# The order of TensorE's products and combines in layers 1 to 4 of a five-layer graph network on one core

## The reference, cut to what matters

```python
x = _layernorm(x + _L0_gnn_ref(x, adj, ...))            # layer 0: adj masked and weighted by rank
def _ggc(x, adj, W, wih, whh, bih, bhh):                # layers 1 and 2
    m = adj @ (x @ W)
    gi = m @ wih.T + bih
    gh = x @ whh.T + bhh
    ...
    r = jax.nn.sigmoid(i_r + h_r); z = jax.nn.sigmoid(i_z + h_z)
    n = jnp.tanh(i_n + r * h_n)
    return (1.0 - z) * n + z * x
x = _layernorm(x + relu(_ggc(relu(_ggc(x, ...)), ...)))
x = _layernorm(x + (dinv[:, None] * (adj + eye) * dinv[None, :]) @ x @ W)          # layer 3
x = _layernorm(x + concat([x, (adj @ x) / deg], -1) @ W.T)                          # layer 4
```

## Time and profile before

| | |
|---|---|
| median of 3 runs | 458.71 us (458.45 to 458.75) |
| time of the profiled execution | 457.77 us |
| its span, first to last instruction | 456.0 us |
| mean granted TensorE clock | 0.985 of full |
| PE busy | 428.1 us, 94% of the span |
| DVE, ACT, POOL busy | 283.2, 197.8, 114.9 us |

### The profile page before, as it was taken

How to read it: one execution, slowest core, us unless ns; L and a number is a source line. 1 busy time by engine, 2 the same in 40 slices (tenths; PEclk the granted TensorE clock), 3 DMA queues, 4 the chain that set the end, 5 groups by cost and what they waited for, 6 DMA issues and landing times.

```text
span 456.0 us, 6313 instructions
## 1 busy us (share of the span) xinstructions
PE 428.1 (94%) x2294; PEld 214.0 (47%) x2294; DVE 283.2 (62%) x777; ACT 197.8 (43%) x335; POOL 114.9 (25%) x155
## 2 busy tenths in 40 slices
PE   5399799999999999999999999999999999999992
PEld 1134244444344444455555545554545655465571
DVE  3575969666964896463667526868742566175453
ACT  2277567766876687506555414445111121100000
POOL 8111614210510020014122111343330444211011
PEclk9889999999999999999999999999999999999997
DMA  8999999999999991000011010000000111101000
GB/s 117 155 163 108 107 107 107 109 113 110 107 110 112 109 99 25 0 7 18 13 24 24 13 23 1 2 1 0 2 0 1 23 24 24 24 12 36 12 13 23
DMA packets 24895, 23.70 MB, mean 52 GB/s; under 512 B 14369, under 2 KB 16289, under 8 KB 24865
## 3 DMA queue, kind: packets, MB, share of 16 engines
q0 software_dynamic: 9360, 16.78, 36.7%
q1 hardware_dynamic: 15216, 6.33, 5.8%
q10 hardware_dynamic: 288, 0.20, 0.2%
HBM read 69.44 MB, written 1.05 MB: 155 GB/s over the span
## 4 chain that ended last, share of the span: by engine, by line
PE 85%; DVE 6%; DMA 3%; ACT 2%; issue 2%; POOL 1%; POOLq 0%; DVEq 0%; ACTq 0%
PE Y L887 46%; PE both L800 17%; PE Y L779 8%; PE Y L791 3%; PE both L760 2%; PE both L763 2%; DMA xrow<-in_xrow 2%; DVE work L550 2%; PE both L755 2%; PE both L766 1%; PE both L807 1%; PE both L768 1%; DMA adjT<-in_adjT 1%; ACT wgt L353 1%; DVE work L555 1%
## 5 line engine op out<-in xcount | busy, mean ns | idle before, releaser
L887 PE MATMUL Y<-adjT,S 128*128 128x512 fp8e4 (+1 forms) x1056 | 232.7, 373 | 1.0 <-POOL S L252 0.7
L887 PEld LDWEIGHTS Y<-adjT,S 128*128 128x128 f16 x1056 | 102.8, 99 | 110.2 <-POOL S L252 1.2
L353 ACT ACTIVATE wgt<-both 128x512 int16<-128x512 f32 x192 | 113.9, 597 | 44.3 <-PE both L800 36.8
L237 POOL TENSOR_TENSOR rstd<-stat,mhalf 128x4 f32<-128x4 f32 (+2 forms) x29 | 34.0, 1173 | 195.0 <-DVE stat L457 195.0
L800 PE MATMUL both<-adjT,fix 128*128 128x512 fp8e4 x192 | 73.8, 384 | 1.0 <-ACT wgt L353 0.5
L800 PE MATMUL both<-adjT,tri 128*128 128x512 fp8e4 x192 | 74.2, 387 | 0.0
L779 PE MATMUL Y<-wgt,S 128*128 128x512 bf16 x192 | 73.8, 384 | 0.0
L265 POOL DMA_DIRECT2D adjT<-in_adjT x63 | 33.7, 570 | 68.3 <-DMA adjT<-in_adjT 68.3
L550 DVE SCALAR_TENSOR_TENSOR work<-work,adjT 128x1024 int16<-128x1024 int16 x32 | 42.7, 1356 | 0.0
L555 DVE SCALAR_TENSOR_TENSOR work<-adjT,work 128x1024 int16<-128x1024 fp8e4 x24 | 29.4, 1225 | 16.7 <-ACT work L350 15.0
L800 PEld LDWEIGHTS both<-adjT,fix 128*128 128x128 bf16 x192 | 18.9, 98 | 38.8 <-ACT wgt L353 17.8
(11 more groups left out here) (112 smaller groups left out, 422.1 us busy)
## 6 DMA issues: line engine op xcount, KB each, us to landing
adjT<-in_adjT POOLq DMA_DIRECT2D x63, 256.0 KB, 39.0
out_rows<-xrow SPq DMA_DIRECT2D x7, 128.0 KB, 1.9
xrow<-in_xrow SPq DMA_DIRECT2D x1, 640.0 KB, 8.7
hrow<-in_w_gates SPq DMA_DIRECT2D x1, 512.0 KB, 13.5
biases<-in_biases SPq DMA_DIRECT2D x1, 416.0 KB, 7.7
x<-S SPq DMA_TRANSPOSE x24, 2.4
xrow<-in_xrow SPq DMA_DIRECT2D x1, 256.0 KB, 4.1
adjT<-in_adjT POOLq DMA_DIRECT2D x2, 128.0 KB, 6.3
```

The source lines that it names most:

```text
L237: nc.gpsimd.tensor_tensor(rstd[:, 0:blocks], stat[:, 2, 0:blocks], mhalf[:, 0:blocks], ALU.pow)\
L353: nc.scalar.activation(wgt[:, c, tiles % 2, :], V[c][:, :], ACT.Relu).then_inc(w_ready[c], 1)
L887: mm = nc.tensor.matmul(bank(layer, g)[:, 0:nb * P], S[layer % 2][:, jb, :], cols[:, jb, :], start=(jb == 0), stop=(jb == JB - 1), skip_gr ...
```

## The change

The four functions that write out PE's order are replaced. The products and combines in them are the same; their order differs.

- In layer 0's tail and the start of layer 1, `combine(0, 6)` comes first and `combine(0, 7)` one slot later, where both stood behind seven slots. `open_gates` comes after 30 more slots instead of 41.
- In layers 1 and 2 each combine of group g stands 13 to 15 slots behind the last slot of the same group's product (19 and 23 for groups 1 and 2 of layer 1); in the kernel before it stands 12 to 66 slots behind. In layer 3 it stands 4 slots behind, with two exceptions at the start, in layer 4 mostly 4 instead of 6.
- At the layer changes two groups (two banks) are open while the last rows of `S` are awaited, and a third is begun, where before three or four groups were open.
- At the end, `combine(4, 6)` and `combine(4, 7)` stand 8 and 6 half-width slots into the next group, where both stood 10.

```diff
             def layer1():
-                product(1, 2, 0, 7)
-                combine(0, G - 2)
-                combine(0, G - 1)
-                product(1, 2, 7, EARLY)
-                product(1, 3, 0, EARLY)
+                combine(0, 6)
+                product(1, 2, 0, 1)
+                combine(0, 7)
+                product(1, 2, 1, 24)
+                product(1, 3, 0, 7)
                 open_gates()
...
+                product(1, 2, 24, 31)
                 combine(1, 0)
-                product(1, 4, 0, 22)
+                product(1, 2, 31, 32)
+                product(1, 3, 9, 20)
                 combine(1, 1)
-                product(1, 4, 22, JB)
-                product(1, 5, 0, 12)
+                product(1, 3, 20, 32)
                 combine(1, 2)
...
+                product(1, 4, 0, 13)
                 combine(1, 3)
+                product(1, 4, 13, 32)
+                product(1, 5, 0, 15)
                 combine(1, 4)
...
             def layer2():
+                product(2, 0, 0, 14)
                 combine(1, 7)
+                product(2, 0, 14, 24)
+                product(2, 1, 0, 12)
+                product(2, 0, 24, 28)
+                product(2, 1, 12, 16)
+                product(2, 0, 28, 32)
+                product(2, 1, 16, 31)
                 combine(2, 0)
+                product(2, 1, 31, 32)
+                product(2, 2, 0, 14)
+                combine(2, 1)
+                product(2, 2, 14, 32)
+                product(2, 3, 0, 14)
+                combine(2, 2)
+                product(2, 3, 14, 32)
+                product(2, 4, 0, 15)
+                combine(2, 3)
...
             def layer3():
-                combine(2, 5)
-                product(3, 0, 0, 20)
-                product(3, 1, 0, 8)
-                combine(2, 6)
-                product(3, 1, 8, 20)
-                product(3, 2, 0, 16)
+                product(3, 0, 0, 14)
                 combine(2, 7)
-                product(3, 2, 16, 20)
-                for g in range(3):
-                    product(3, g, 20, 24)
-                product(3, 3, 0, 24)
-                for g in range(4):
-                    product(3, g, 24, 28)
-                for g in range(4):
-                    product(3, g, 28, JB)
+                product(3, 0, 14, 24)
+                product(3, 1, 0, 21)
+                product(3, 0, 24, 28)
+                product(3, 1, 21, 28)
+                product(3, 2, 0, 11)
+                product(3, 0, 28, 32)
+                product(3, 1, 28, 32)
                 combine(3, 0)
                 combine(3, 1)
...
             def layer4():
...
+                product(4, 7, 0, 8)
+                combine(4, 6)
+                product(4, 7, 8, 32)
+                product(4, 8, 0, 6)
+                combine(4, 7)
+                product(4, 8, 6, 32)
                 combine(4, 8)
```

More of the change, by code:

```diff
@@ L920, in layer1 @@
-                product(1, 3, EARLY, JB)
+                product(1, 3, 7, 9)
+                product(1, 0, 24, 32)
+                product(1, 1, 24, 32)
+                product(1, 2, 24, 31)
                 combine(1, 0)
-                product(1, 4, 0, 22)
+                product(1, 2, 31, 32)
+                product(1, 3, 9, 20)
                 combine(1, 1)
-                product(1, 4, 22, JB)
-                product(1, 5, 0, 12)
+                product(1, 3, 20, 32)
                 combine(1, 2)
-                product(1, 5, 12, JB)
@@ L928, in layer1 @@
-                product(1, 6, 0, 2)
+                product(1, 4, 0, 13)
                 combine(1, 3)
-                product(1, 6, 2, 24)
+                product(1, 4, 13, 32)
+                product(1, 5, 0, 15)
                 combine(1, 4)
-                product(1, 6, 24, JB)
-                product(1, 7, 0, 14)
+                product(1, 5, 15, 32)
+                product(1, 6, 0, 15)
                 combine(1, 5)
-                product(1, 7, 14, JB)
+                product(1, 6, 15, 32)
@@ L937, in layer2 @@
+                product(1, 7, 0, 15)
+                combine(1, 6)
+                product(1, 7, 15, 32)
             def layer2():
[L939 to L942, removed]
+                product(2, 0, 0, 14)
                 combine(1, 7)
[L944 to L948, removed]
@@ L949, in layer2 @@
-                for g in range(3):
-                    product(2, g, 28, JB)
-                product(2, 3, 0, 4)
-                combine(2, 0)
[L953 to L958, removed]
-            def layer3():
-                combine(2, 5)
-                product(3, 0, 0, 20)
-                product(3, 1, 0, 8)
-                combine(2, 6)
-                product(3, 1, 8, 20)
-                product(3, 2, 0, 16)
-                combine(2, 7)
-                product(3, 2, 16, 20)
-                for g in range(3):
-                    product(3, g, 20, 24)
-                product(3, 3, 0, 24)
-                for g in range(4):
-                    product(3, g, 24, 28)
-                for g in range(4):
-                    product(3, g, 28, JB)
-                product(3, 4, 0, 8)
+                product(2, 0, 14, 24)
@@ new lines, in layer2 @@
+                combine(2, 3)
+                product(2, 4, 15, 32)
+                product(2, 5, 0, 15)
+                combine(2, 4)
+                product(2, 5, 15, 32)
+                product(2, 6, 0, 15)
+                combine(2, 5)
+                product(2, 6, 15, 32)
+                product(2, 7, 0, 15)
+                combine(2, 6)
+                product(2, 7, 15, 32)
+            def layer3():
+                product(3, 0, 0, 14)
+                combine(2, 7)
+                product(3, 0, 14, 24)
[5 more added lines that the diff above has]
+                product(3, 1, 28, 32)
@@ L978, in layer3 @@
                 combine(3, 0)
-                product(3, 4, 8, 28)
                 combine(3, 1)
-                product(3, 4, 28, JB)
-                product(3, 5, 0, 16)
+                product(3, 2, 11, 32)
+                product(3, 3, 0, 4)
                 combine(3, 2)
-                product(3, 5, 16, JB)
-                product(3, 6, 0, 3)
+                product(3, 3, 4, 32)
+                product(3, 4, 0, 4)
                 combine(3, 3)
-                product(3, 6, 3, 22)
+                product(3, 4, 4, 32)
@@ L988, in layer3 @@
+                product(3, 5, 0, 4)
                 combine(3, 4)
-                product(3, 6, 22, JB)
-                product(3, 7, 0, 9)
+                product(3, 5, 4, 32)
+                product(3, 6, 0, 4)
                 combine(3, 5)
-                product(3, 7, 9, 28)
+                product(3, 6, 4, 32)
+                product(3, 7, 0, 4)
                 combine(3, 6)
-                product(3, 7, 28, JB)
+                product(3, 7, 4, 32)
             def layer4():
-                product(4, 0, 0, 20)
+                product(4, 0, 0, 4)
@@ L999, in layer4 @@
                 combine(3, 7)
[L1000 to L1006, removed]
+                product(4, 0, 4, 28)
+                product(4, 1, 0, 7)
+                product(4, 0, 28, 32)
+                product(4, 1, 7, 11)
                 combine(4, 0)
-                product(4, 2, 14, JB)
+                product(4, 1, 11, 32)
@@ L1009, in layer4 @@
+                product(4, 2, 0, 4)
                 combine(4, 1)
[L1010 to L1015, removed]
+                product(4, 2, 4, 32)
+                product(4, 3, 0, 4)
+                combine(4, 2)
+                product(4, 3, 4, 32)
+                product(4, 4, 0, 4)
@@ new lines, in layer4 @@
+                combine(4, 3)
+                product(4, 4, 4, 32)
+                product(4, 5, 0, 4)
+                combine(4, 4)
+                product(4, 5, 4, 32)
+                product(4, 6, 0, 4)
+                combine(4, 5)
+                product(4, 6, 4, 32)
+                product(4, 7, 0, 8)
[4 more added lines that the diff above has]
+                product(4, 8, 6, 32)
+                combine(4, 8)
```

1 line of the change is left out of this document (removed).

## The result

| | before | changed |
|---|---|---|
| median of 4 runs each | 458.73 us (458.45 to 458.75) | 460.67 us (460.36 to 460.99) |
| time of the profiled execution | 457.77 us | 460.64 us |
| its span | 456.0 us | 458.8 us |
| from layer 0's last copy to DVE's last line 463 | 257.46 us | 259.44 us |

A forecast was written before the change was run, and what follows sets the result against it. PE's own work was taken to set the time of layers 1 to 4. Two waits removed, slots lost and the tail, -1.42 + 2.15 - 0.22 = +0.5 us, on 458.71 gave 459.2 us, range 457.9 to 460.3.

The forecast's parts named there:

- the prediction's own signs of being wrong: New gap over 1 us, S late at another layer change, line 663 under 0.7 us behind 476, or clock falling.
- What the two waits hold, 1.42: PE's waits for DVE's m_lo ahead of combine(2, 0) and POOL's S in layer 3 hold 0.52 and 0.90 us.
- The lag, 3.29 us: Layers 1 and 2: from a group's last slot to its combine takes 3.29 us, 15.2 slots.
- Its disputed step: DVE, line 476 to the start of 663: taken as 0.72 us from 482 to 672; other bound 0.61.
- Layer 3 adds nothing: Layer 3: ACT's copy chain of 0.82 to 0.94 us against 4 slots of 0.86 costs nothing; other bound 0.5.
- The collision at layer 2 to 3, 0.45: POOL's lines 289 and 247 meet DVE's 672 to 674 of group 7; half of 2 x 0.47 us taken.
- Start of layer 1, 0.3: DVE's work on groups 0 and 1 makes combine(1, 3) late; 0.3 us lost in all.
- nothing at layer changes 0 to 1, 1 to 2 and 3 to 4: Rows PE needs there come in time, so no loss; 0 to 1 fits by 0.24, 3 to 4 by 0.3 us.
- The tail, -0.22: combine(4, 6) comes 2 half-width slots earlier and DVE is the chain to the end; gain 0.22 us.
- the lag is longer, at every group: Rival: ACT's copy takes 0.69 us to DVE's start; 3.6 added, +1.9, 460.6 us; chance 0.23.
- Everything fits: Rival: shorter hand-over, 663 follows 476 in 0.61, POOL's lines don't collide; -1.4, 457.3 us; chance 0.1.

The follow-up runs named there:

- l12_15: Changed kernel with combines (1,7), (2,1), (2,2) and (2,7) 15 slots behind their products instead of 14; 459.98 us, 1.0030 of the kernel before.
- l12_16: Changed kernel with combines of layers 1 and 2 from (1,4) on, except (2,0), 16 slots behind their products instead of 14 or 15; 459.45 us.
- l3_five: Changed kernel with 5 slots instead of 4 between product and combine for combines (3,2) to (3,7); 459.97 us, 1.0026 of the kernel before.
- l3_three: Changed kernel with 3 slots instead of 4 between product and combine for combines (3,2) to (3,7); 461.91 us, 1.0073 of the kernel before.
- no_meet: Changed kernel with POOL's lines 289 and 247 writing a constant for group 6 of layer 2, so they don't read SBUF; 459.98 us.
- tail: Kernel before with the changed tail alone, combines (4,6) and (4,7) behind 8 and 6 half-width slots instead of 10; 458.46 us, ratio 1.0000.
- all_fit: Changed kernel with product-to-combine distances just long enough in layers 1 to 3 and 15 slots ahead of the last rows of S; 457.37 us, 0.9968 of before.

## Why the prediction was wrong

The direction was right, and so was the mechanism of layers 1 and 2. The size was not: layer 3 stood in the sum at nothing, and the collision was sized at half. None of the prediction's own signs of being wrong showed (the new gap is 0.51 on the page, line 663 starts 0.73 behind 476, the granted clock didn't fall, and `S` is late at no other layer change), because none of them looked at layer 3's combines. By its own steps:

- **What the two waits hold, 1.42.** Right: both are gone, and with nothing lost elsewhere the kernel gains it back.
- **The lag, 3.29 us.** Right. 15 slots lose 0.05 and 14 lose 0.27, and 16 lose nothing (`l12_15`, `l12_16`). Its disputed step is in the trace of after, a timeline of DVE at group 6 of layer 2:

```profile
318.76 0.69 DVE L476 SCALAR_TENSOR_TENSOR work<-Y,yT 64x512 f32<-64x512 f32 x1 [1.96 <-ACT yT L315]
319.49 0.49 DVE L663 SCALAR_TENSOR_TENSOR work<-both,rz 128x128 f32<-128x128 f32 x2
```

  Line 663 starts 0.73 behind line 476, not 0.61. The forecast's 0.72, taken over from the step between lines 482 and 672, was right to 0.01. What makes these two steps longer than the 0.61 from line 522 to 514 no run shows.
- **Layer 3 adds nothing: this is the step that failed.** The forecast had the copy's chain at 0.82 to 0.94 us against four slots of 0.86, took nothing, and had 0.5 as the other bound. The chain is 0.95 (352.52 - 351.57), at the upper bound or just over it, since the hand-over to PE is 0.15 (352.52 - 352.37). That makes 0.09. The bound itself was too small, because it counted only a later start. A combine that waits also has its first weight load in the open, 0.07 more. 0.16 at six combines is 0.96, and the pair (3,0), (3,1) adds 0.18: 1.14 in place of 0. `l3_five` and `l3_three` show that this is the distance and nothing else. This one term is about three quarters of the error, and the same load costs the 0.08 at `combine(0, 6)`. In layer 4, also costed at nothing, nothing was lost.
- **The collision at layer 2 to 3, 0.45.** It came where it was forecast, on lines 672 and 673, but whole: 0.72. I took half of the bound because the first overlap is partial. It is (0.30), yet the second isn't shorter for it; line 674, which the forecast named too, stayed plain (0.48). Layer 2 to 3 lost 0.94 in place of 0.7, a term mis-sized by 0.24. `no_meet` shows the cause. The hand-over from POOL to PE goes the other way: 0.05 (334.61 to 334.66) where the forecast took 0.15.
- **Start of layer 1, 0.3**, and nothing at layer changes 0 to 1, 1 to 2 and 3 to 4: right (0.34, and no wait there).
- **The tail, -0.22**: right, -0.23, and -0.22 in `tail`, by the trace alone.
- **The rivals.** The time that "the lag is longer, at every group" gave, 460.6, is the one that came, but by luck and not by its mechanism: the groups of layers 1 and 2 lost 0.05 at 15 slots and 0.27 at 14, where this rival had 0.12 and 0.34. "Everything fits" described a kernel that had to be written differently, `all_fit`.

Corrected with 1.14, 0.24, 0.08 and 0.04 more, the sum is +0.5 + 1.50 = +2.0, against 1.98 in the traces and 1.94 in the medians.

## What to carry to other kernels

When an order puts a consumer just behind its producer, a margin that comes out within a tenth of a microsecond of the cover is to be costed at its upper bound, and multiplied by how often it recurs: here one to three slots more at each combine, and four ahead of the last rows of `S`, turned +1.9 us into -1.4. For a matmul that waits for its operand, count the weight load that can no longer run ahead (0.07 us here) as well as the later start (0.09). Small recurrent gaps (up to 0.29 us here) don't show in a list of waits or in idle time; compare the distance of the same instruction in successive groups with bare work.

## What the runs showed of the hardware

- A fp32 combine of 8 matmuls, 64 columns each, takes PE 0.84 us when its first weight load starts 0.16 to 0.21 ahead of it, and 0.91 to 0.92 when the load stands 0.03 ahead, whether it had waited 0.09 us, 0.29 us or not at all (layer 4). For the fp16 combines of layers 1 and 2 no such cost shows: 1.32 where the combine waited (288.11 to 289.43) and 1.32 in `l12_16`, where it didn't (287.06 to 288.38).
- PE started 0.15 us behind ACT's end in layer 3, the same as behind DVE's in the earlier trace rows, and 0.05 behind POOL's (334.61 to 334.66); ACT's end to DVE's start took 0.03 in the earlier trace rows.
- DVE's lines 672 and 673, which met POOL's SBUF reads in a row, paid 0.30 and 0.41 us (0.79 and 0.90 against 0.49); in `no_meet`, with POOL's memsets of the same size (0.31 each, 0.42 us of them beside line 672) in place of those reads, they paid nothing.
- PE's gaps of up to 0.67 us, and one of 0.05 to 0.27 in most stretches of 8.3 us, left the granted clock where it was: 0.99 from 193 us on, in the kernel before and in the changed one.
